# Second attention of a two-layer decoder: keys by blocks of 64 on two partition halves, sinks in a bank of their own

## The reference

```python
# L1 attention: 4 batches, 256 tokens, 16 heads of 16, window 64, 4 sink keys
q = (x @ Wq.T);  latent = x @ Wkv_down.T
k = latent @ Wk_up.T;  v = latent @ Wv_up.T
att = einsum('bhqd,bhkd->bhqk', q, k) / sqrt(16)
mask = (j <= i) & (j >= i - 63)  |  (j < 4) & (j <= i)      # i query, j key
att = softmax(where(mask, att, -inf))
y = einsum('bhqk,bhkd->bhqd', att, v) @ Wo.T
```

## Time and profile before

| What | Value |
|---|---|
| median of 3 runs | 509.61 us (508.43 to 509.75) |
| profiled execution, its own time | 509.1 us |
| span of that execution | 507.4 us |
| second attention's front, until its back starts | about 253 to 297.8 us of the span |
| second attention's back | 297.8 to about 385 us |
| PE busy over the span | 404.9 us (80%) |

### The profile page before, as it was taken

The page is one execution under the profiler, slowest core; times in us unless marked ns, Lnnn a source line. Parts: engine busy times, 40 slices in busy tenths (PEclk is TensorE's granted clock), DMA queues, the critical chain, the costliest instruction groups (busy, mean ns, idle before and its releaser), DMA issues.

```text
span 507.4 us, 8072 instructions
## 1 busy us (share of the span) xinstructions
PE 404.9 (80%) x3090; PEld 315.9 (62%) x3090; DVE 349.4 (69%) x802; ACT 239.8 (47%) x420; POOL 99.1 (20%) x103
## 2 busy tenths in 40 slices
PE   1906478998884664599998688999986899999993
PEld 1506445676653552388766565666765788888883
DVE  0489698777877968476648879656946485666545
ACT  1558714665433653466567713546536324422220
POOL 4400005439401030051183000000002700000000
PEclk9967598999997757579999989999999899999998
DMA  6900020000000000000000005970000000000101
GB/s 203 295 6 1 1 70 5 3 3 2 2 2 0 1 1 0 0 1 1 1 1 1 1 1 79 122 150 3 1 2 1 0 1 1 0 1 1 43 1 41
DMA packets 13125, 13.32 MB, mean 26 GB/s; under 512 B 2904, under 2 KB 12448, under 8 KB 12832
## 3 DMA queue, kind: packets, MB, share of 16 engines
q1 hardware_dynamic: 12224, 12.54, 11.0%
q10 hardware_dynamic: 864, 0.27, 0.2%
HBM read 11.56 MB, written 1.05 MB: 25 GB/s over the span
## 4 chain that ended last, share of the span: by engine, by line
PE 62%; DVE 21%; ACT 11%; issue 3%; DMA 1%; POOL 1%; SPq 0%; DVEq 0%; POOLq 0%; ACTq 0%
PE PS L2135 12%; PE PS L2152 6%; ACT arena L743 6%; PE PS L1750 4%; PE PS L1834 4%; DVE mx L1250 3%; PE PS L1728 3%; PE PS L2062 3%; PE PS L2075 3%; PE PS L1875 3%; PE PS L381 3%; PE PS L1802 2%; PE PS L1844 2%; PE PS L1631 2%; PE PS L1782 2%
## 5 line engine op out<-in xcount | busy, mean ns | idle before, releaser
L862 ACT ACTIVATE PT<-PS 128x512 f32<-128x512 f32 x96 | 53.5, 594 | 36.0 <-PE PS L1802 35.9
L2135 PE MATMUL PS<-arena_r 128*128 128x512 f32 x264 | 66.0, 399 | 2.2 <-ACT xT L743 2.2
L664 POOL TENSOR_SCALAR va<-mv 128x4 f32<-128x4 f32 x12 | 5.3, 441 | 274.9 <-DVE mv L1086 274.9
L743 ACT ACTIVATE arena<-PS 96x1024 bf16<-96x1024 bf16 (+4 forms) x59 | 44.4, 807 | 27.7 <-PE PS L1728 12.9
L2135 PEld LDWEIGHTS PS<-arena_r 128*128 128x128 f32 x264 | 49.2, 193 | 12.2 <-issue 2.6
L1728 PE MATMUL PS<-ident,arena 128*96 128x128 bf16 x416 | 32.3, 249 | 28.8 <-DVE arena L1129 27.5
L1728 PEld LDWEIGHTS PS<-ident,arena 128*96 128x96 bf16 x416 | 30.5, 148 | 32.5 <-DVE arena L1129 29.1
L1750 PE MATMUL PS<-masks,ident 128*128 128x512 bf16 x112 | 43.0, 384 | 4.7 <-DVE mx L1250 2.4
L1250 DVE TENSOR_REDUCE mx<-PS 128x4 f32<-128x1024 f32 x32 | 39.0, 1220 | 1.2 <-PE PS L1782 0.2
L2152 PEld LDWEIGHTS PS<-arena_r 128*128 128x128 f32 x264 | 34.4, 191 | 2.5 <-DVE arena_r L1553 0.9
L2152 PE MATMUL PS<-arena_r 128*128 128x256 f32 x264 | 35.1, 283 | 0.7 <-DVE arena_r L1553 0.7
(11 more groups left out here) (218 smaller groups left out, 904.1 us busy)
## 6 DMA issues: line engine op xcount, KB each, us to landing
arena<-in_L_ffn_w SPq DMA_DIRECT2D x16, 176.0 KB, 9.6
arena<-in_L_ffn_w SPq DMA_DIRECT2D x2, 1024.0 KB, 11.1
arena<-in_L_ffn_w SPq DMA_DIRECT2D x2, 704.0 KB, 6.2
arena<-in_fside_BxS2xS SPq DMA_DIRECT2D x1, 1024.0 KB, 12.3
out<-x SPq DMA_DIRECT2D x4, 256.0 KB, 2.6
x<-in_x SPq DMA_DIRECT2D x1, 768.0 KB, 8.7
arena<-in_L_attn_Wq SPq DMA_DIRECT2D x2, 256.0 KB, 4.4
arena<-in_L_attn_Wo SPq DMA_DIRECT2D x2, 256.0 KB, 6.5
```

Of the source, the lines that this page charges most:

```text
L743: return nc.scalar.activation(dst, src, ACT.Copy)
L862: nc.scalar.activation(PT[:, n % 2, 512 * j:512 * (j + 1)], bank(3 + j), ACT.Exp, scale=NEG_SCALE)\
L2135: last = mm(bank(2 * (n % 2) + gu), wp[c][:, gu, c_ * P:(c_ + 1) * P], xp[5][:, c, blk * 512:(blk + 1) * 512], start=(step == 0 and c == 0 ...
```

## The change

The causal branch, which the first attention uses, stays. For the second attention:

- `exp_scores`: banks 3 and 4 still get a mask of 512 columns (from a new table `chunk_mask`), but the keys go by blocks of 64: block c writes partitions 0 to 63 (c even) or 64 to 127 (c odd) and only the 128 queries that may see it (64 for the last). That is four matmuls a head, eight a bank. Bank 5 now holds only the sinks of queries 128 to 255, four heads on four strips of 32 partitions and 128 columns, after a mask of 128 columns (`sink_rows`).
- `exponentials`: the third one reads 128 columns instead of 512.
- `windowed_values` replaces the two rows of matmuls by four: blocks 0 and 1 (128 columns), a middle block whose values `V_mid` lie with keys 128 to 191 on partitions 0 to 63 and 64 to 127 on 64 to 127 (64 columns), the last block (64 columns), and the sinks (`V_sink`, 4 rows, 128 columns).
- GpSimd builds `sink_rows` and `chunk_mask` (5 memsets, 4 copies) behind the long memset, and `V_mid` (8 copies of 64x512, in the words of `xb`) as soon as the values exist (`v_ready`).
- SP issues 16 small DMAs that fill `V_sink`, ahead of the first rows of maxima (`mrow_dmas`).

```diff
+            sp.wait_ge(A[1]["v_ready"], TT)
+            for i in range(HG):
+                for b in range(B):
+                    sp.dma_start(V_sink[32 * i:32 * i + SINK, b, :, :], V1[0:SINK, 2 * b, i::HG, :]).then_inc(v_sink_loaded, 16)
             mrow_dmas(sp, 1, 0)
...
+            alone(pool.memset(sink_rows[:, :], -1.0e30), window_set)
+            for i in range(HG):
+                alone(pool.memset(sink_rows[32 * i:32 * i + SINK, :], 0.0), window_set)
+            alone(pool.tensor_copy(chunk_mask[:, 0:P], masks[:, 1, 3 * P:4 * P]), window_set)
...
+            pool.wait_ge(A[1]["v_ready"], TT)
+            for b in range(B):
+                alone(pool.tensor_copy(V_mid[0:WIN, b], V1[0:WIN, 2 * b + 1]), window_set)
+                alone(pool.tensor_copy(V_mid[WIN:P, b], V1[WIN:P, 2 * b]), window_set)
...
+                cols = P if L == 1 and j == 2 else 512
+                nc.scalar.activation(PT[:, n % 2, 512 * j:512 * j + cols], bank(3 + j, cols), ACT.Exp, scale=NEG_SCALE)\
...
+                            for c in range(4):
+                                lo, hi = c * WIN, min(c + 2, 4) * WIN
+                                last = mm(PS[WIN * (c % 2):WIN * (c % 2) + WIN, bk, q0 + lo:q0 + hi], K_[0:R, b, h, lo:lo + WIN],
+                                          Qh[0:R, b, h, lo:hi], start=False, stop=(i == 1 and c >= 2))
...
-                        mask(bank(5), slice(5 * P, 6 * P), HG, True)
+                        mm(bank(5, P), ident16[:, :], sink_rows[:, 0:1].to_broadcast([P, P]), start=True, stop=False)
...
+                            last = mm(PS[32 * i:32 * i + 32, 5, 0:P], K_[0:R, b, h, 0:32], Qh[0:R, b, h, P:S],
+                                      start=False, stop=True)
...
+                def windowed_values(b, g, j, ob):
+
+                    e = PT[:, j % 2, 0:1024].rearrange("p (h s) -> p h s", h=HG)
+                    es = PT[:, j % 2, 1024:1024 + P]
+                    sources = ((0, 2, V1[:, 2 * b]), (2, 3, V_mid[:, b]), (3, 4, V1[:, 2 * b + 1]))
+                    for lo, hi, v_ in sources:
+                        for i in range(HG):
+                            mm(PS[VW * i:VW * (i + 1), ob, lo * WIN:hi * WIN], v_[:, HG * g + i, :],
+                               e[:, i, lo * WIN:hi * WIN], start=(lo == 0), stop=False)
+                    for i in range(HG):
+                        last = mm(PS[VW * i:VW * (i + 1), ob, P:S], V_sink[32 * i:32 * i + SINK, b, g, :],
+                                  es[32 * i:32 * i + SINK, :], start=False, stop=True)
+                    last.then_inc(A[1]["av"], 1)
```

More of the change, by code:

```diff
@@ L66, in post_ln_decoder_two_layers @@
         exponents = sb("exponents", [P, 2, B * DC])
+        V_sink = sb("V_sink", [P, B, NG, VW])
+        sink_rows = sb("sink_rows", [P, 1], BF16)
+        chunk_mask = sb("chunk_mask", [P, S], BF16)
         stat = sb("stat", [P, 4, 6])
@@ L167, in post_ln_decoder_two_layers @@
         PT_words = PT[:, :, :].rearrange("p a b -> p (a b)")
+        V_mid = xb[:, :, :].rearrange("p a b -> p (a b)").rearrange("p (b h d) -> p b h d", b=B, h=H)
         xb_words = xb[:, :, :].rearrange("p a b -> p (a b)")
@@ L713, in _ @@
             alone(pool.memset(Kh[MROW:MROW + 3, :, :, :].rearrange("p a b c -> p (a b c)"), -1.0), krow_set)
+            pool.wait_ge(w["tables"], LOADS["tables"])
+            alone(pool.memset(sink_rows[:, :], -1.0e30), window_set)
+            for i in range(HG):
+                alone(pool.memset(sink_rows[32 * i:32 * i + SINK, :], 0.0), window_set)
+            alone(pool.tensor_copy(chunk_mask[:, 0:P], masks[:, 1, 3 * P:4 * P]), window_set)
+            alone(pool.tensor_copy(chunk_mask[0:WIN, P:P + WIN], masks[0:WIN, 1, 5 * P:5 * P + WIN]), window_set)
+            alone(pool.tensor_copy(chunk_mask[WIN:P, P:P + WIN], masks[WIN:P, 1, 4 * P:4 * P + WIN]), window_set)
+            alone(pool.tensor_copy(chunk_mask[:, P + WIN:S], masks[:, 1, 5 * P + WIN:6 * P]), window_set)
+            pool.wait_ge(A[1]["v_ready"], TT)
+            for b in range(B):
+                alone(pool.tensor_copy(V_mid[0:WIN, b], V1[0:WIN, 2 * b + 1]), window_set)
+                alone(pool.tensor_copy(V_mid[WIN:P, b], V1[WIN:P, 2 * b]), window_set)
             inverse_deviations(3, 0)
@@ L1743, in attn_back @@
                 pe.wait_ge(krow_set, L + 1)
+                if L == 1:
+                    pe.wait_ge(window_set, 1 + HG + 4)
                 def kv(h):
@@ L1798, in exp_scores @@
                         if not causal:
-                            mask(bank(bk), slice(3 * P, 5 * P), 2, True)
+                            mm(bank(bk), ident16[:, :], chunk_mask[:, :].unsqueeze(1).to_broadcast([P, 2, S]), start=True, stop=False)
                         for i in range(2):
                             h = HG * g + 2 * j + i
-                            last = mm(bank(bk, S, i * S), K_[0:R, b, kv(h), 0:P], Qh[0:R, b, h, :],
-                                      start=(causal and i == 0), stop=(i == 1))
+                            q0 = i * S
+                            if causal:
+                                last = mm(bank(bk, S, q0), K_[0:R, b, kv(h), 0:P], Qh[0:R, b, h, :],
+                                          start=(i == 0), stop=(i == 1))
+                                continue
+                            for c in range(4):
+                                lo, hi = c * WIN, min(c + 2, 4) * WIN
+                                last = mm(PS[WIN * (c % 2):WIN * (c % 2) + WIN, bk, q0 + lo:q0 + hi], K_[0:R, b, h, lo:lo + WIN],
+                                          Qh[0:R, b, h, lo:hi], start=False, stop=(i == 1 and c >= 2))
                         last.then_inc(a["sT"], 1)
@@ L1807, in exp_scores @@
                     if not causal:
-                        mask(bank(5), slice(5 * P, 6 * P), HG, True)
+                        mm(bank(5, P), ident16[:, :], sink_rows[:, 0:1].to_broadcast([P, P]), start=True, stop=False)
                     for i in range(HG):
                         h = HG * g + i
-                        last = mm(bank(5, P, i * P), K_[0:R, b, kv(h), P:S], Qh[0:R, b, h, P:S],
-                                  start=(causal and i == 0), stop=(i == HG - 1))
-                    last.then_inc(a["sT"], 1)
+                        if causal:
+                            last = mm(bank(5, P, i * P), K_[0:R, b, kv(h), P:S], Qh[0:R, b, h, P:S],
+                                      start=(i == 0), stop=(i == HG - 1))
+                        else:
+                            last = mm(PS[32 * i:32 * i + 32, 5, 0:P], K_[0:R, b, h, 0:32], Qh[0:R, b, h, P:S],
+                                      start=False, stop=True)
+                    last.then_inc(a["sT"], 1)
+                def windowed_values(b, g, j, ob):
[10 more added lines that the diff above has]
+                    last.then_inc(A[1]["av"], 1)
                 def values(j):
@@ L1830, in values @@
                     ob = output_bank(j)
+                    if not causal:
+                        if j == 0:
+                            pe.wait_ge(window_set, 1 + HG + 4 + 2 * B)
+                            pe.wait_ge(v_sink_loaded, 16 * B * HG)
+                        windowed_values(b, g, j, ob)
+                        return
                     p0 = PT[:, j % 2, 0:1024].rearrange("p (h s) -> p h s", h=HG)
```

4 lines of the change are left out of this document (3 added, 1 removed).

## The result

The changed kernel took 526.04 us (median of 4 runs, 522.88 to 529.24), the kernel before beside it 509.68 (4 runs, 508.43 to 512.53): ratio 1.0304, 95% interval 1.0252 to 1.0356. That is slower, as forecast, but by 16 us where I had 5.8, and outside my range of 509.5 to 521. The profiled execution took 525.26 us with a span of 523.5, for 509.1 and 507.4 before: 16.1 us of span to account for. Executions of every kernel here, the one before too, may come out some 5 us longer by delays ahead of 160 us of the span, a part that no change touches, so the profiles' periods from group to group decide more than a median does.

The account below looks back on a forecast made before the run. TensorE was taken to bound the second attention's back. The profiled 509.1 us plus 4.1 (TensorE), 1.5 and 0.2 (GpSimd's copies delaying VectorE) gave 514.9 us, with 8 in 10 for 509.5 to 521.

Parts of the forecast that it names:

- The shapes: TensorE's second attention: each change of stationary shape costs 0.09 to 0.10 us; a bank 0.66, a group +0.245 us.
- halves side by side: Banks 3 and 4: upper and lower 64-partition matmuls run together, two heads 0.22 us; rival that they queue, 12 in 100.
- GpSimd: Front: V_mid copies delay VectorE's four L1129, +1.5 us; four earlier copies +0.2; back's start moves by 1.7.
- The front's clock: Front: late transposes might stay at the lower clock level, up to +0.8 us, not in the sum.
- SP and ScalarE: SP's 16 small DMAs, about 9.5 us with 2.3 us of room, and ScalarE's shorter third exponential: both 0.
- The step that failed: Pricing each group's banks, values and sinks on TensorE by columns and shape changes: +0.245 us a group, +4.1 us together.
- The direction: Whole kernel: slower by over 0.3%, 0.86; within 0.07; faster 0.07.
- the sum: Whole kernel: 509.1 + 4.1 + 1.5 + 0.2 = 514.9 us.
- TensorE cannot be fed: Rival, back's narrow matmuls: 0.041 us each at the fastest, +0.63 us a group, 525.0 us; 5 in 100.

Follow-up runs that it names:

- e3: Changed kernel with the masks of all three banks ahead of the scores, three changes of shape fewer in a group: 526.16 us, ratio 1.0293.
- e8: Changed kernel with masks first, V_mid copies later, weight loads paced, and sinks' values zero-padded to 128 rows: 508.17 us, ratio 0.9906 to the kernel before.
- e5: Changed kernel whose GpSimd V_mid copies wait until VectorE's last L1154 is done: 524.14 us, ratio 1.0282.
- e10: Changed kernel run once more as it was, for a second profile: 525.04 us, ratio 1.0244.
- e1: Changed kernel with each expert up weight load cut to 8 elements a row, so queues stay nearly empty: 516.77 us, ratio 1.0101.
- e4: Changed kernel with all weight loads spread, later pairs waiting for a group's scores, and V_sink DMAs issued earlier: 518.31 us, ratio 1.0196.
- e2: Kernel before with the second attention's matmuls split into 448 more over the same columns, no new shape: 519.83 us, ratio 1.0172.
- e9: Kernel before with 448 more matmuls over the same columns and expert up weight loads cut to 8 elements a row: 509.46 us, ratio 0.9953.
- e11: e8 run once more as it was, for a second profile: 507.12 us, ratio 0.9953.
- e6: Kernel before with the expert up weight loads cut to 8 elements a row, as a control: 510.65 us, ratio 1.0027.

## Why the prediction was wrong

**The shapes.** Right in mechanism and size: 0.24 for 0.245 a group, 0.65 for 0.66 a bank, halves side by side. e3 and e8 measured a change of shape apart, 0.11 us each. One thing needs narrowing: between 96, 99 and 128 rows nothing is paid (a mask and L1809 follow each other at 0.22 us), only for fewer.

**GpSimd.** The mechanism is shown by e5, the size was off: 0.4 us for 1.5; with the early copies the whole front is 0.6 longer at an equal stretch of lower clock (e10), for a forecast of 1.7. I had each L1129 wait for a whole copy; in the trace mostly the copy was held up (1.49 for 0.61) and VectorE lost 0.1 an instruction.

**The front's clock.** I named it, bounded it at 0.8 and left it out of the sum. It cost 1.2 to 1.4 us in one profile of the changed kernel and nothing in the other. Whether that is chance is open: in the five profiles with the early copies (the changed kernel's two, e1, e3, e4) the clock was low for 6.8 us three times and 3.4 twice, in the eight without them (before, e2, e5 to e9, e11) for 3.4 four times and never in the other four.

**SP and ScalarE.** 0, as said: TensorE did not wait for the small DMAs, though their 11.00 us used up all of the room and the first rows of maxima left 0.16 us late.

**The step that failed** is the change part by part, where it priced TensorE's new instructions by their columns and shapes alone. The direction came out as forecast, but of the 16 us only about 4 are terms of the sum (3.7 in the periods, 0.4 to 0.6 in the front). 448 more matmuls are also 448 more pairs of instructions to be brought from memory (q8's 28 blocks for 25), and in the earlier trace rows the DMA share of 0.81 in the very stretch of steps 2 and 3 was a number that I showed and didn't use. The rival "TensorE cannot be fed" (5 in 100, 525.0 us) came near the time by luck, with another mechanism: it made every narrow matmul slow, +0.63 a group. No period shows that, and in e1 and e9, with the same matmuls, nothing is slow. What the runs show in its place is two pauses of about 2 us each and a lower clock in or behind them, 8.1 us together in the first profile and 13.1 in the second: TensorE runs through a block in 7.4 us where it took 12.0, and the next one lands only after 7.9, with 1.8 more until TensorE goes on. They need both more instructions (e2 has them with the old shapes, the kernel before with the same loads doesn't) and full queues (e1 and e9 don't have them, nor has e4 with the same bytes spread). Four corners, two kernels and two loads, agree.

**Open.** That the stream ran dry is read from the late block, the count of 256 and the four corners, since the trace has no record of a sequencer out of instructions; what the block's packet waits for among the loads, and what the 1.3 to 2.0 us behind its landing are, no run shows. That the lower clock follows from a pause isn't shown: it stood in or within 1.3 us behind eight of the ten pauses, and never between the first and the last group's start without one, but e2's second pause, 3.3 us of idle time, and e5's second, 1.0, have none behind them; nothing made a pause of another kind. The 1.7 us behind the last group's start are hardly the change's: the stretch from there to the end took 138.0 and 139.3 us in the two profiles of the changed kernel and 136.3 before, but 135.4 in e5, which is the changed kernel there, and 137.4 in e6, which is the kernel before; over all profiles it runs from 135.4, with no lower clock in it up to 500 us, to 139.9, with 10.2 us of it, and I have no cause for that number.

## What to carry to other kernels

Count a change's instructions as bytes that must arrive, and look at the DMA share in the stretch where they run. Compare how long the engine takes over 256 instructions with how late a block comes there: where the queues are full, many small matmuls can cost more than their columns, and pacing the loads by the consumer's progress gives it back. A gain on the busy engine shows nothing while such a wait ends the stretch (e3), so take the wait away first and measure the gain again. And pay for a change of shape as seldom as possible: put the matmuls of one shape together, or pad the contraction with zero rows, since rows cost nothing in e8 and a change 0.11 us.

## What the runs showed of the hardware

- TensorE's instructions come in blocks of 256 (packets of 16384 bytes; 28 of them for 7276 records), and with nearly empty queues a block's packet starts within 0.8 us of the start of the block ahead of it (e1, e9) or up to 1.8 us before it (e6).
- Behind loads that filled the queues such a packet started 6.9 us behind that point instead of 0.2 (e2, e9), and TensorE stood idle for 1.0 to 3.4 us in ten pauses of five profiles, always behind the same two records, 4033 and 4289.
- In or right behind eight of these ten pauses the granted clock was at 1.2 GHz, for stretches of 3.4 to 13.7 us; behind a pause of 3.3 us in e2 it stayed at 2.4.
- A change of the stationary operand from 128 columns to 64 or 32, or from 128 rows to 4, costs about 0.11 us of TensorE also where nothing waits (e3, e8); between 96, 99 and 128 rows there is no such cost.
- Matmuls on partitions 0 to 63 and 64 to 127 run side by side: 896 named columns in 0.34 us with a change of shape in it, the time of 512.
- GpSimd's copy of 64x512 float32 took 0.61 us, a `V_sink` DMA 0.69 us of SP's queue to issue.
